# Moving small VectorE and GpSimd work between the eight steps of a round in a gated attention and expert kernel

## The chip, the cores and the metric

The kernel runs on one core of one Trainium2 chip. The metric is the device time of one launch in microseconds (us). The core has five engines that work from their own queues and wait for each other only at semaphores: TensorE (PE in the profile, with its weight loads shown as PEld), VectorE (DVE), ScalarE (ACT), GpSimd (POOL) and the sync engine (SP), which here only issues DMAs.

## What is computed

Each of 32 batches has 256 tokens of 128 features. Attention with a gated recurrent state comes first, then a feed-forward layer with one shared expert and eight routed ones, of which each token takes two. Both are modulated by a condition vector.

```python
h = layernorm(x) * (1 + ca) + sa
q, k, v = h @ W_q, h @ W_k, h @ W_v           # 16 heads of 64
a = sigmoid(h @ W_gate + b_gate)
# per head, token by token:
S = a_t[..., None] * S + k_t[..., None] * v_t[..., None, :]
o_t = einsum('bhk,bhkv->bhv', q_t, S)
x = x + ga * (o @ W_o)
h = layernorm(x) * (1 + cb) + sb
probs = sigmoid(h @ router_w.T + routing_bias)
scores, indices = top_k(probs, 2);  scores = scores / scores.sum()
x = x + gb * (shared_expert(h) + sum over the 2 chosen experts of score * expert(h))
```

## The kernel before

The program has two parts. The first, up to about 1000 us, does the attention of all batches and, behind it, the routing; the second multiplies the routed rows by the experts and adds everything up. The change touches the first part alone.

The first part is a loop over 16 rounds of two batches each. A round has eight **steps** (s = 0 to 7, `DUOS` = 4 to a batch); step number d = 8 i + s handles four heads of one batch. Rounds 0 to 2 and 15 are written out, and rounds 3 to 14 are one hardware loop. Each engine has its own function `round_of_steps`, and the order of its lines is the order in which that engine works: nothing reorders it. So a small operation that stands ahead of a large one delays it even where another engine waits for the large one.

What each engine does in a step s, in order:

- **PE**: `attend(d-1)` (the masked scores times the values, into `vo_bank`), `scores(d)` (into `score_banks`), the gate projection for step d+2 (`z_bank`), then in some steps a small product in `vo_bank` (the router in s = 0, transposes of the normalised input in s = 1 and 5, `ranks` in s = 4, transposes of the routed rows `new_rows` in s = 6 and 7), the query and key projections for step d+1 (`qk_banks`), `values` into `vo_bank`, and the output projection (`y_bank`).
- **DVE**: `first_head(d)` (two masked copies of scores into `A`, lines 1196 and 1198), `products(d+1)` (two multiplications of `qk_banks` by the scans, line 1188) and `scans(d+2)` (lines 1176 and 1181). Small work stands between them: `normalise`, `split_h` and `moments` for a coming batch, `moments2` and `normalise2` for the routed rows `new_rows`, and the routing of the two batches of the round before: `logits`, `choose`, `weigh`, `places`.
- **POOL**: `mask_second_head(d)` (the causal mask on the second head's half of `A`, line 510), `growth(d+1)` (line 600) and `gates(d+2)` (lines 593 and 595). Small work: `inverse_std`, `logits_exp`, `update_x`, `h_rows` (three operations on `new_rows` of one batch, from line 567) and `scatter_rows` (line 584: one indirect DMA for each of the eight parts of a round's routed rows).
- **ACT** copies PSUM results out, computes the gate's exponentials, and copies the second head's scores to `A`, behind which POOL masks them.

These waits of PE matter here. `attend(d-1)` waits until `first_head(d-1)` and `mask_second_head(d-1)` are done. `scores(d)` waits for `products(d)`. In s = 4 `values` overwrites `vo_bank`, in which the ranks lie, so it waits for `s_pos`, which DVE signals at line 1160, the second operation of `places`. In s = 6 and 7 the transposes wait for `h_rows`. On the other side `scatter_rows` waits for `s_dest`, the end of `places`, and `gates(d+2)` waits for `scans(d+1)`.

The lines of DVE that set the order in steps 3 to 5 are these (before):

```python
first_head(d)
if s == 3 and two:
    choose(i - 1)
if s == 5 and one:
    for u in range(2):
        normalise2((i - 1) * 2 + u, u, i)
if e == 0 and more:
    normalise(b * CHUNKS + CHUNKS, s_rs, b + 2, s_xn)
...
if s == 4 and two:
    places(i - 1)
if not (last and s == 2 * DUOS - 1):
    products(d + 1)
```

Of the kernel before, what the change touches and what calls it, by code (L numbers as in the profile page):

```python
# [20 lines left out]
ROUNDS = B // 2  # L21
# [21 lines left out]
def block_kernel(nc, x, W_q, W_k, W_v, W_gate, b_gate, W_o, shared_gate, shared_up, shared_down,  # L43
# [11 lines left out]
    with ctx:  # L55
# [442 lines left out]
        def _(pool):  # L498
# [120 lines left out]
            def round_of_steps(i, last):  # L619
                one = not (isinstance(i, int) and i < 1)  # L620
                two = not (isinstance(i, int) and i < 2)
                three = not (isinstance(i, int) and i < 3)
                for s in range(2 * DUOS):
                    half, e = s // DUOS, s % DUOS
                    b, d = i * 2 + half, i * 2 * DUOS + s
                    if e == 0 and not (last and half == 1):
                        inverse_std(b + 2)
                    if s == 0 and three:
                        scatter_rows(i - 2, s_fill, (i - 2) * 16, (6, 7))
                    if s in (1, 2) and two:  # L630
                        for n in range(2):
                            logits_exp(i - 1, (s - 1) * 2 + n)
                    if e == 3 and (half == 1 or one):
                        update_x(b - 1)
                    if s == 4 and one:
                        inverse_std2(i)
                    if s == 6 and one:
                        h_rows((i - 1) * 2 + 1, i - 1, 1, i)
                    if s >= 5 and two:
                        scatter_rows(i - 1, s_fill, (i - 1) * 16, ((0, 1), (2, 3), (4, 5))[s - 5])  # L640
                    mask_second_head(d)
                    if not (last and s == 2 * DUOS - 1):
                        growth(d + 1)
                    if not (last and s >= 2 * DUOS - 2):
                        gates(d + 2)
                    if s == 5 and one:
                        h_rows((i - 1) * 2, i - 1, 0, i)

            inverse_std(1)
            pool.wait_ge(s_wsplit, 4)  # L650
# [9 lines left out]
            with pool.Fori(3, ROUNDS - 1) as i:  # L660
                round_of_steps(i, False)
            round_of_steps(ROUNDS - 1, True)
            scatter_rows(ROUNDS - 2, s_fill, (ROUNDS - 2) * 16, (6, 7))
            update_x(B - 1)
            logits_exp(ROUNDS - 1, 0)
            inverse_std2(ROUNDS)
# [321 lines left out]
        def _(dve):  # L988
# [10 lines left out]
            def alone(semaphore, count):  # L999


                count = count if isinstance(count, int) else dve.to_reg(count)
                dve.wait_ge(s_ident, 1)
                dve.wait_ge(semaphore, count)  # L1004
# [142 lines left out]
                chosen(k, 6)  # L1147
                v.tensor_tensor(picked[:, :, :], pick[:, 0, :, :], pick[:, 1, :, :], ALU.add).then_inc(s_pick, 1)

            def places(k, where=dest):  # L1150

                def step(count):
                    alone(s_pl, (k - 1) * 3 + count)

                alone(s_rk, k)
                v.tensor_tensor(place_e[:, :, :], RANK[:, 0:PT * E].rearrange("p (n e) -> p n e", n=PT),
                                next_row[:, :].rearrange("p (a e) -> p a e", a=1).broadcast_to([P, PT, E]),
                                ALU.add).then_inc(s_pl, 1)
                step(1)
                v.tensor_tensor(next_row[:, :], next_row[:, :], RANK[:, PT * E:(PT + 1) * E], ALU.add).then_inc(s_pos, 1)  # L1160
                for t in range(TOP):
                    ins = v.tensor_tensor(place_k[:, t, :, :], pick[:, t, :, :], place_e[:, :, :], ALU.mult)
                ins.then_inc(s_pl, 1)
                step(2)
                v.tensor_reduce(place_f[:, :, :], place_k[:, :, :, :], AX.X, ALU.add).then_inc(s_pl, 1)
                step(3)
                alone(s_e0, k)
                v.tensor_copy(where[:, :], place_f[:, :, :].rearrange("p t n -> p (t n)")).then_inc(s_dest, 1)

            def scans(d):  # L1170

# [28 lines left out]
            def round_of_steps(i, last):  # L1200
                one = not (isinstance(i, int) and i < 1)
                two = not (isinstance(i, int) and i < 2)
                for s in range(2 * DUOS):
# [1 line left out]
                    b, d = i * 2 + half, i * 2 * DUOS + s  # L1205
                    more = not (last and half == 1)
                    first_head(d)
                    if s == 3 and two:
                        choose(i - 1)
                    if s == 5 and one:  # L1210
                        for u in range(2):
                            normalise2((i - 1) * 2 + u, u, i)
                    if e == 0 and more:
                        normalise(b * CHUNKS + CHUNKS, s_rs, b + 2, s_xn)
                    if s == 0 and two:
                        logits(i - 1)
                    if e == 1 and more:
                        split_h((1 - half) * T, b + 2)
                    if s == 4 and two:
                        places(i - 1)  # L1220
                    if not (last and s == 2 * DUOS - 1):
                        products(d + 1)
                    if s == 3 and two:
                        weigh(i - 2, i - 1)
                    if s == 3 and one:
                        moments2(b - 1, 1, i)
                    if s == 7:
                        moments2(b - 1, 0, i + 1)
                    if e == (3 if isinstance(b, int) and b == 0 else 2) and not last:
                        if isinstance(b, int) and b == 0:  # L1230
                            dve.wait_ge(s_x_rest, 16)
                        moments(b * CHUNKS + 2 * CHUNKS, b + 3)
# [703 lines left out]
```

## Time and profile before

| what | us |
|---|---|
| median of three timed runs (1334.47 to 1336.96) | 1336.66 |
| the profiled execution's own time | 1335.02 |
| its span, first to last instruction | 1332.9 |
| PE busy in the span | 1209.7 (91%) |
| DVE busy | 1039.1 (78%) |
| POOL busy | 946.5 (71%) |
| ACT busy | 717.1 (54%) |

Busy shares are means over both parts of the program. What a delay costs is seen only where an engine sits idle, in the round itself; the rows for that stand further down. A timeline row gives the start and the duration of one instruction, or of a few merged ones (x16), and in square brackets how long its engine had been idle before it and whose work ended the wait. Merged rows of pipelined instructions can overlap by a tenth of a microsecond.

### The profile page before, as it was taken

What the parts mean: (1) busy time and instruction counts of PE and PEld (TensorE: products, weight loads), DVE (VectorE), ACT (ScalarE), POOL (GpSimd) and SP (SyncE); (2) the same over time, 40 slices, a digit from 0 to 9 for tenths busy, and PEclk for the clock granted to TensorE, in tenths of its full rate; (3) what the DMA queues carried; (4) which work ended last, traced back from release to release, by engine and by line L of the source; (5) the groups of instructions that cost most, each with busy time, mean ns of one, the idle gap of its engine ahead of it and who ended that gap; (6) DMA issues with size and microseconds to landing.
All of it is one profiled execution on the core that took longest, in us unless ns stands there. A gap on an engine that the chain in (4) does not pass through costs nothing. (4 is left out here: it accounts for less than half of the span.)

```text
span 1332.9 us, 35442 instructions
## 1 busy us (share of the span) xinstructions
PE 1209.7 (91%) x10935; PEld 1063.2 (80%) x10935; DVE 1039.1 (78%) x2183; ACT 717.1 (54%) x1637; POOL 946.5 (71%) x1288
## 2 busy tenths in 40 slices
PE   5999999999999999998999999999989799999960
PEld 5888878888888878787888888887878688898850
DVE  7778788787878788888878787878766478887767
ACT  4666656556555556555555655655645345445420
POOL 4336687768696968778786969686876457777754
PEclk9999999999999999999999999999999999999995
DMA  8810202021120202020202112020202266666146
GB/s 247 240 69 2 90 22 87 25 85 58 47 98 7 101 8 97 10 95 20 85 24 85 63 42 101 4 101 8 99 26 92 70 189 193 191 178 182 61 155 224
DMA packets 88445, 119.30 MB, mean 90 GB/s; under 512 B 9652, under 2 KB 52327, under 8 KB 88384
## 3 DMA queue, kind: packets, MB, share of 16 engines
q1 hardware_dynamic: 79296, 101.47, 23.7%
q0 software_dynamic: 9088, 17.07, 3.7%
q8 instruction: 31, 0.51, 0.2%
q14 instruction: 30, 0.25, 0.1%
HBM read 50.29 MB, written 61.79 MB: 84 GB/s over the span
## 5 line engine op out<-in xcount | busy, mean ns | idle before, releaser
L1188 DVE TENSOR_TENSOR pairs<-qk_banks,pairs 128x512 f32<-128x512 f32 x256 | 164.5, 684 | 82.0 <-PE qk_banks L1537 81.5
L1638 PE MATMUL vo_bank<-A,shared 128*64 128x256 f32 (+1 forms) x2048 | 197.0, 335 | 27.5 <-POOL A L510 26.7
L710 POOL DMA_INDIRECT y_dram<-pairs,y_row x156 | 158.2, 1014 | 68.2 <-issue 43.9
L1176 DVE TENSOR_TENSOR_SCAN pairs<-pairs,shared 128x515 f32<-128x515 f32 x128 | 174.2, 1361 | 36.3 <-POOL pairs L593 30.1
L510 POOL TENSOR_SCALAR_AFFINE_SELECT A<-A 128x256 f32<-128x256 f32 x256 | 100.0, 416 | 136.3 <-ACT A L786 136.1
L1623 PE MATMUL score_banks<-pairs 64*128 64x128 f32 x2048 | 193.1, 286 | 3.2 <-ACT kx L779 3.2
L1638 PEld LDWEIGHTS vo_bank<-A,shared 128*64 128x64 f32 x2048 | 129.3, 138 | 81.7 <-issue 24.0
L1181 DVE TENSOR_TENSOR_SCAN pairs<-pairs,shared 128x515 f32<-128x515 f32 x128 | 167.8, 1311 | 0.0
L1623 PEld LDWEIGHTS score_banks<-pairs 64*128 64x128 f32 x2048 | 147.0, 189 | 25.7 <-issue 25.7
L584 POOL DMA_INDIRECT rows_dram<-token_rows,dest x120 | 124.9, 1041 | 58.3 <-issue 31.5
L767 ACT ACTIVATE shared<-vo_bank 128x512 f32<-128x512 f32 x128 | 76.5, 598 | 165.0 <-PE vo_bank L1638 165.0
L1535 PE MATMUL qk_banks<-h_hi,big 128*128 128x256 f32 x512 | 151.8, 297 | 0.0
L1537 PE MATMUL qk_banks<-h_hi,big 128*128 128x256 f32 x512 | 144.3, 282 | 0.0
L1649 PEld LDWEIGHTS y_bank<-wo,shared 128*128 128x128 f32 x1024 | 133.8, 191 | 13.1 <-ACT h_tile L792 1.1
L1536 PE MATMUL qk_banks<-h_lo,big 128*128 128x256 f32 x512 | 144.1, 281 | 0.0
L1649 PE MATMUL y_bank<-wo,shared 128*128 128x128 f32 x1024 | 135.1, 275 | 1.6 <-ACT h_tile L792 0.9
L758 ACT ACTIVATE shared<-vo_bank 128x512 f32<-128x512 f32 x128 | 76.5, 598 | 104.5 <-PE vo_bank L1580 104.5
L576 POOL TENSOR_TENSOR lg_e<-inv_e,lg 128x8 f32<-128x8 f32 x64 | 119.2, 1876 | 9.3 <-DVE lg L1115 9.3
L1196 DVE COPY_PREDICATED A<-causal,score_banks 128x512 f32<-128x512 int32 x128 | 93.7, 732 | 29.1 <-PE score_banks L1623 26.7
L746 ACT ACTIVATE pairs<-z_bank,neg_bg 128x256 f32<-128x256 f32 x256 | 107.6, 473 | 6.6 <-PE z_bank L1537 2.9
L785 ACT ACTIVATE A<-score_banks 128x256 f32<-128x256 f32 x128 | 49.2, 385 | 114.4 <-PE score_banks L1623 114.4
L752 ACT ACTIVATE pairs<-z_bank,half_bg 128x256 f32<-128x256 f32 x256 | 108.4, 486 | 0.0
(252 smaller groups left out, 3163.9 us busy)
## 6 DMA issues: line engine op xcount, KB each, us to landing
rows_dram<-pad_row SPq DMA_DIRECT2D x17, 2112.0 KB, 8.1
ga_all<-rows_dram SPq DMA_DIRECT2D x39, 264.0 KB
pairs<-y_dram SPq DMA_DIRECT2D x16, 512.0 KB
pairs<-in_L_ffn_gate_w_dram SPq DMA_DIRECT2D x39, 128.0 KB
pairs<-in_L_ffn_up_w_dram SPq DMA_DIRECT2D x39, 128.0 KB
ga_all<-in_L_ffn_down_w_dram SPq DMA_DIRECT2D x39, 128.0 KB, 2.2
mod_rows<-mod_rows_dram SPq DMA_DIRECT2D x32, 128.0 KB, 3.1
h_all<-h_tile SPq DMA_DIRECT2D x16, 256.0 KB, 2.3
```

The costliest lines, as they stand in the source:

```text
L576: g.tensor_tensor(lg_e[:, n, :], inv_e[:, n, :], lg[:, n, :], ALU.pow).then_inc(s_le, 1)
L584: g.indirect_dma_start(rows_dram, bass.IndirectOffsetOnAxis(ap=places[:, m:m + 1], axis=0), rows[:, m % PT, :], None, bounds_check=ROWS - ...
L710: g.indirect_dma_start(y_dram, bass.IndirectOffsetOnAxis(ap=y_row[:, u, n:n + 1], axis=0), y_out[:, u, n, :], None, bounds_check=TOKENS * ...
L1176: v.tensor_tensor_scan(G[:, 0:WIDE - 1], gi_t[:, 0:WIDE - 1], cap[:, 0:WIDE - 1], 1.0, ALU.mult, ALU.min)
L1181: v.tensor_tensor_scan(F[:, 0:WIDE - 1], ga_t[:, 0:WIDE - 1], restart[:, 0:WIDE - 1], 1.0, ALU.mult, ALU.add).then_inc(s_fg, 1)
L1188: v.tensor_tensor(out[:, :, :].rearrange("p u (c t) -> p u c t", c=CHUNKS), QKS[:, :, off:off + T].rearrange("p u (c t) -> p u c t", c=CHU ...
L1535: t.matmul(dst, hi, m_hi, start=True, stop=False)
L1536: t.matmul(dst, hi, m_lo, start=False, stop=False)
L1537: return t.matmul(dst, lo, m_hi, start=False, stop=True)
L1623: last = t.matmul(S[:, first:first + P], keys[rows, :], queries[rows, :], start=True, stop=True)
L1638: last = t.matmul(VO[h * DK:(h + 1) * DK, u * T + k * P:(u + 1) * T], v_sb[:, k, vcols], blocks.rearrange("p c t -> p (c t)"), start=(k == ...
L1649: last = t.matmul(Y[:, k * D:(k + 1) * D], oT[:, u * T + k * P:u * T + (k + 1) * P], wo[:, 2 * e + u, :], start=(e == 0 and u == 0 and k = ...
```

## The change

It moves work; no operation is added or left out, and a round still has eight scatters.

- On DVE, `places` is split into `rank_rows` (the two operations that read the ranks in PSUM and signal `s_pos`) and `destinations` (the rest). In s = 4 `rank_rows` stands right behind `first_head`, and `destinations` behind `products`. `normalise` and `split_h` go behind `products`, `logits` ahead of it. `choose` goes from s = 3, ahead of `products`, to s = 2, behind `products`. `normalise2` is split: one batch in s = 5 and the other in s = 6. `moments` for the first batch goes from s = 2 to s = 1.
- On POOL, the scatters, which stood two each in s = 5, 6, 7 and the next round's 0, are now three in s = 5, two in s = 6, none in s = 7, two in the next s = 0 and one in s = 1. `h_rows` of the second batch goes from the beginning of s = 6, ahead of the mask, to its end, behind the gates.
- Behind the last round three scatters are left in place of two.

The order of PE, ACT and SP is the same, instruction for instruction.

```diff
@@ -625,8 +625,8 @@
                     b, d = i * 2 + half, i * 2 * DUOS + s
                     if e == 0 and not (last and half == 1):
                         inverse_std(b + 2)
-                    if s == 0 and three:
-                        scatter_rows(i - 2, s_fill, (i - 2) * 16, (6, 7))
+                    if s < 2 and three:
+                        scatter_rows(i - 2, s_fill, (i - 2) * 16, ((5, 6), (7,))[s])
                     if s in (1, 2) and two:
                         for n in range(2):
                             logits_exp(i - 1, (s - 1) * 2 + n)
@@ -634,17 +634,15 @@
                         update_x(b - 1)
                     if s == 4 and one:
                         inverse_std2(i)
-                    if s == 6 and one:
-                        h_rows((i - 1) * 2 + 1, i - 1, 1, i)
-                    if s >= 5 and two:
-                        scatter_rows(i - 1, s_fill, (i - 1) * 16, ((0, 1), (2, 3), (4, 5))[s - 5])
+                    if s in (5, 6) and two:
+                        scatter_rows(i - 1, s_fill, (i - 1) * 16, ((0, 1, 2), (3, 4))[s - 5])
                     mask_second_head(d)
                     if not (last and s == 2 * DUOS - 1):
                         growth(d + 1)
                     if not (last and s >= 2 * DUOS - 2):
                         gates(d + 2)
-                    if s == 5 and one:
-                        h_rows((i - 1) * 2, i - 1, 0, i)
+                    if s in (5, 6) and one:
+                        h_rows((i - 1) * 2 + s - 5, i - 1, s - 5, i)
 
             inverse_std(1)
             pool.wait_ge(s_wsplit, 4)
@@ -660,7 +658,7 @@
             with pool.Fori(3, ROUNDS - 1) as i:
                 round_of_steps(i, False)
             round_of_steps(ROUNDS - 1, True)
-            scatter_rows(ROUNDS - 2, s_fill, (ROUNDS - 2) * 16, (6, 7))
+            scatter_rows(ROUNDS - 2, s_fill, (ROUNDS - 2) * 16, (5, 6, 7))
             update_x(B - 1)
             logits_exp(ROUNDS - 1, 0)
             inverse_std2(ROUNDS)
@@ -1147,17 +1145,20 @@
                 chosen(k, 6)
                 v.tensor_tensor(picked[:, :, :], pick[:, 0, :, :], pick[:, 1, :, :], ALU.add).then_inc(s_pick, 1)
 
-            def places(k, where=dest):
-
-                def step(count):
-                    alone(s_pl, (k - 1) * 3 + count)
+            def rank_rows(k):
 
                 alone(s_rk, k)
                 v.tensor_tensor(place_e[:, :, :], RANK[:, 0:PT * E].rearrange("p (n e) -> p n e", n=PT),
                                 next_row[:, :].rearrange("p (a e) -> p a e", a=1).broadcast_to([P, PT, E]),
                                 ALU.add).then_inc(s_pl, 1)
-                step(1)
+                alone(s_pl, (k - 1) * 3 + 1)
                 v.tensor_tensor(next_row[:, :], next_row[:, :], RANK[:, PT * E:(PT + 1) * E], ALU.add).then_inc(s_pos, 1)
+
+            def destinations(k, where=dest):
+
+                def step(count):
+                    alone(s_pl, (k - 1) * 3 + count)
+
                 for t in range(TOP):
                     ins = v.tensor_tensor(place_k[:, t, :, :], pick[:, t, :, :], place_e[:, :, :], ALU.mult)
                 ins.then_inc(s_pl, 1)
@@ -1166,6 +1167,10 @@
                 step(3)
                 alone(s_e0, k)
                 v.tensor_copy(where[:, :], place_f[:, :, :].rearrange("p t n -> p (t n)")).then_inc(s_dest, 1)
+
+            def places(k, where=dest):
+                rank_rows(k)
+                destinations(k, where)
 
             def scans(d):
 
@@ -1205,28 +1210,29 @@
                     b, d = i * 2 + half, i * 2 * DUOS + s
                     more = not (last and half == 1)
                     first_head(d)
-                    if s == 3 and two:
-                        choose(i - 1)
-                    if s == 5 and one:
-                        for u in range(2):
-                            normalise2((i - 1) * 2 + u, u, i)
+                    if s == 0 and two:
+                        logits(i - 1)
+                    if s == 4 and two:
+                        rank_rows(i - 1)
+                    if s in (5, 6) and one:
+                        normalise2((i - 1) * 2 + s - 5, s - 5, i)
+                    if not (last and s == 2 * DUOS - 1):
+                        products(d + 1)
+                    if s == 4 and two:
+                        destinations(i - 1)
                     if e == 0 and more:
                         normalise(b * CHUNKS + CHUNKS, s_rs, b + 2, s_xn)
-                    if s == 0 and two:
-                        logits(i - 1)
                     if e == 1 and more:
                         split_h((1 - half) * T, b + 2)
-                    if s == 4 and two:
-                        places(i - 1)
-                    if not (last and s == 2 * DUOS - 1):
-                        products(d + 1)
+                    if s == 2 and two:
+                        choose(i - 1)
                     if s == 3 and two:
                         weigh(i - 2, i - 1)
                     if s == 3 and one:
                         moments2(b - 1, 1, i)
                     if s == 7:
                         moments2(b - 1, 0, i + 1)
-                    if e == (3 if isinstance(b, int) and b == 0 else 2) and not last:
+                    if s == (6 if half else 3 if isinstance(b, int) and b == 0 else 1) and not last:
                         if isinstance(b, int) and b == 0:
                             dve.wait_ge(s_x_rest, 16)
                         moments(b * CHUNKS + 2 * CHUNKS, b + 3)
```

DVE, in rounds 3 to 14, from the `products` of step 2 to those of step 4, before (`lg_e` to `tsum` is `choose`, `place_e` and `next_row` are the ranks' reads, `dest` ends `places`, lines 1196 and 1198 are `first_head`):

```order
L1188 TENSOR_TENSOR pairs<-qk_banks,pairs 128x512 x2
...
L1124 TENSOR_SCALAR lg<-lg_e 128x32
...
L1134 TENSOR_TENSOR tsum<-top 128x4
L1188 TENSOR_TENSOR pairs<-qk_banks,pairs 128x512 x2
...
L1198 COPY_PREDICATED A<-causal,score_banks 128x256
L1020 TENSOR_SCALAR xn<-xs,mv,rstd 128x128 x2
L1156 TENSOR_TENSOR place_e<-vo_bank,next_row 128x32
L1160 TENSOR_TENSOR next_row<-next_row,vo_bank 128x8
...
L1168 CAST dest<-place_f 128x8
L1188 TENSOR_TENSOR pairs<-qk_banks,pairs 128x512 x2
```

and now:

```order
L1193 TENSOR_TENSOR pairs<-qk_banks,pairs 128x512 x2
L1122 TENSOR_SCALAR lg<-lg_e 128x32
...
L1132 TENSOR_TENSOR tsum<-top 128x4
...
L1193 TENSOR_TENSOR pairs<-qk_banks,pairs 128x512 x2
...
L1203 COPY_PREDICATED A<-causal,score_banks 128x256
L1151 TENSOR_TENSOR place_e<-vo_bank,next_row 128x32
L1155 TENSOR_TENSOR next_row<-next_row,vo_bank 128x8
L1193 TENSOR_TENSOR pairs<-qk_banks,pairs 128x512 x2
...
L1169 CAST dest<-place_f 128x8
```

`choose` has moved behind the `products` of step 2, the reads of the ranks stand directly behind `first_head`, and `normalise` has left the place between them.

POOL, in the same rounds, from the scatters of step 5 to the mask of step 7, before (`new_rows<-token_ids` begins an `h_rows`, `y_sb` and `xs` are `update_x`, `AFFINE_SELECT` is the mask):

```order
L584 DMA rows_dram<-token_rows,dest 73216x132 x2
...
L510 AFFINE_SELECT A<-A 128x2x128 x2
...
L567 COPY new_rows<-token_ids 128x2
...
L584 DMA rows_dram<-token_rows,dest 73216x132 x2
...
L510 AFFINE_SELECT A<-A 128x2x128 x2
...
L617 TENSOR_TENSOR xs<-xs,y_sb 128x256
L584 DMA rows_dram<-token_rows,dest 73216x132 x2
...
L510 AFFINE_SELECT A<-A 128x2x128 x2
```

and now:

```order
L584 DMA rows_dram<-token_rows,dest 73216x132 x3
...
L510 AFFINE_SELECT A<-A 128x2x128 x2
...
L567 COPY new_rows<-token_ids 128x2
...
L584 DMA rows_dram<-token_rows,dest 73216x132 x2
...
L510 AFFINE_SELECT A<-A 128x2x128 x2
...
L567 COPY new_rows<-token_ids 128x2
...
L617 TENSOR_TENSOR xs<-xs,y_sb 128x256
...
L510 AFFINE_SELECT A<-A 128x2x128 x2
```

Ahead of the mask of step 5 there is one scatter more; the second `h_rows` (in the first list it stands right behind the one shown, among the rows left out) has crossed the mask of step 6; and ahead of the mask of step 7 there is `update_x` alone.

## Rows read from the trace of the kernel before

**Rows 1.** Waits, all of PE: line, waited for, us, times, longest us.

```profile
PE vo_bank L1638 <- POOL A L510: 26.7, 27, 2.4
PE vo_bank L1578 <- DVE next_row L1160: 25.0, 14, 2.2
```

**Rows 2.** Windows, one round: length, busy us of each engine, clock, DMA.

```profile
497.10:558.70 61.60, 57.78 (x579) 50.77 (x577) 50.20 (x105) 36.20 (x89) 47.80 (x69) 1.00 0.16 57
```

**Rows 3.** Timeline of PE, `attend` at the steps' starts: start, duration, [idle].

```profile
528.28 1.52 PE L1638 MATMUL vo_bank<-A,shared 128*64 128x256 f32 x16
535.19 1.52 PE L1638 MATMUL vo_bank<-A,shared 128*64 128x256 f32 x16
...
542.81 0.50 PE L1578 MATMUL vo_bank<-big,h_hi 128*128 128x512 f32 x1 [1.94 <-DVE next_row L1160]
544.59 1.52 PE L1638 MATMUL vo_bank<-A,shared 128*64 128x256 f32 x16
...
551.73 1.52 PE L1638 MATMUL vo_bank<-A,shared 128*64 128x256 f32 x16
...
560.17 1.52 PE L1638 MATMUL vo_bank<-A,shared 128*64 128x256 f32 x16 [1.25 <-POOL A L510]
...
568.01 1.52 PE L1638 MATMUL vo_bank<-A,shared 128*64 128x256 f32 x16 [0.64 <-POOL A L510]
575.81 1.52 PE L1638 MATMUL vo_bank<-A,shared 128*64 128x256 f32 x16
...
582.95 1.30 PE L1638 MATMUL vo_bank<-A,shared 128*64 128x256 f32 x12
```

**Rows 4.** Timeline of DVE, steps 2 to 4 of the same round.

```profile
526.90 1.29 DVE L1188 TENSOR_TENSOR pairs<-qk_banks,pairs 128x512 f32<-128x512 f32 x2 [1.28 <-PE qk_banks L1537]
...
529.08 1.34 DVE L1176 TENSOR_TENSOR_SCAN pairs<-pairs,shared 128x515 f32<-128x515 f32 x1
...
532.42 0.41 DVE L1124 TENSOR_SCALAR lg<-lg_e 128x32 f32<-128x32 f32 x1
...
534.56 1.28 DVE L1188 TENSOR_TENSOR pairs<-qk_banks,pairs 128x512 f32<-128x512 f32 x2
...
540.21 0.72 DVE L1196 COPY_PREDICATED A<-causal,score_banks 128x512 f32<-128x512 int32 x1
...
541.14 1.25 DVE L1020 TENSOR_SCALAR xn<-xs,mv,rstd 128x128 f32 x2
...
542.59 0.16 DVE L1160 TENSOR_TENSOR next_row<-next_row,vo_bank 128x8 f32<-128x8 f32 x1
```

**Rows 5.** Timeline of POOL, from step 5 to the next round's step 1.

```profile
544.46 1.09 POOL L584 DMA_INDIRECT rows_dram<-token_rows,dest  x1 [2.14 <-DVE dest L1168]
...
548.71 0.77 POOL L510 TENSOR_SCALAR_AFFINE_SELECT A<-A 128x256 f32<-128x256 f32 x2 [1.88 <-ACT A L786]
...
551.45 0.18 POOL L567 COPY new_rows<-token_ids 128x2 f32 x1
...
556.85 1.04 POOL L584 DMA_INDIRECT rows_dram<-token_rows,dest  x1 [0.25 <-issue]
...
559.16 0.77 POOL L510 TENSOR_SCALAR_AFFINE_SELECT A<-A 128x256 f32<-128x256 f32 x2
...
561.23 1.69 POOL L614 TENSOR_TENSOR y_sb<-y_sb,ga_all 128x256 f32<-128x256 f32 x1
...
566.99 0.79 POOL L510 TENSOR_SCALAR_AFFINE_SELECT A<-A 128x256 f32<-128x256 f32 x2
...
569.17 1.03 POOL L549 TENSOR_SCALAR veps<-mv 128x2 f32<-128x2 f32 x1
...
576.61 4.20 POOL L576 TENSOR_TENSOR lg_e<-inv_e,lg 128x8 f32<-128x8 f32 x2
...
583.05 3.33 POOL L576 TENSOR_TENSOR lg_e<-inv_e,lg 128x8 f32<-128x8 f32 x2
```

**Rows 6.** Tile `dest`, all scatters from it: duration ns min/median/max.

```profile
L584 POOL DMA_INDIRECT rows_dram<-token_rows,dest x120: 966/1010/1952, 173.7 to 1043.6; - x120
```

## Prediction

> **What bounds the kernel now.** I read the waits of PE first, since PE is the busiest engine. Two waits stand out: the causal mask of the second head, from POOL, holds `attend` up for 26.7 us in 27 places, and the ranks' read, from DVE, holds `values` up for 25.0 us in 14 places [rows 1]. Together they are 51.7 us. Then I read one round in windows: it lasts 61.6 us, of which PE works 57.8, DVE 50.2 and POOL 47.8 [rows 2]. So PE bounds the round, with holes, and a hole that is closed shortens the round as long as DVE and POOL keep up. The timeline of PE shows where the holes are: 1.94 us in step 4, 1.25 at the beginning of step 7 (the mask of step 6 is late) and 0.64 at the beginning of the next step 0 (the mask of step 7) [rows 3]. That is 3.83 us a round. A reader should see in the same rows how long a step takes without its hole: 6.91 us for step 3, 9.40 - 1.94 = 7.46 for step 4, 7.14 for step 5, 8.44 - 1.25 = 7.19 for step 6, 7.84 - 0.64 = 7.20 for step 7, 7.80 for step 0 and 7.14 for step 1. These are the deadlines against which the moved work is set.
>
> **The ranks' read on DVE.** PE wants to go on at 542.81 - 1.94 = 540.87, which is 5.68 us into step 4; the read ends at 542.59 + 0.16 = 542.75 [rows 3, 4]. `first_head` ends where `normalise` begins, at 541.14. `normalise` then takes 1.25 us, with the two reads behind it [rows 4]. Taking it away alone gives an end near 541.14 + 0.44 = 541.58, so 0.7 us of the wait would stay. The rest has to come from `choose`. It takes 534.56 - 532.42 = 2.14 us ahead of the `products` of step 3 [rows 4]. In step 2 it now stands behind `products`, which end at 526.90 + 1.29 = 528.19. There it replaces `moments`, which took until 529.08, so the scans begin at 530.33, or 1.25 us later, and `first_head` of step 3 ends at 532.42 + 1.25 = 533.67. PE has the next projection ready one step after 526.90, at 533.81. So `products` of step 3 start at 533.81 in place of 534.56, and all behind them comes 0.75 us earlier. `first_head` of step 4 ends at 540.39, the reads at 540.83, and PE wants them at 540.87. This closes the wait with nothing to spare; if `choose` takes longer there, as it may beside other POOL work, the excess over 533.81 - 533.67 = 0.14 comes back in every round.
>
> **The masks on POOL.** Ahead of the mask of step 6 POOL now does two scatters and no `h_rows`, ahead of that of step 7 `update_x` without scatters, but the mask of step 5 gets three scatters, and step 1 one. POOL has little rest here, so I add up the whole row of work in the new order, with durations from its timeline [rows 5]: a scatter is half of 559.16 - (556.85 - 0.25) = 2.56, so 1.28; a mask 0.77, and mask, growth and gates together 561.23 - 559.16 = 2.07, or 569.17 - 566.99 = 2.18 in step 7 and after; an `h_rows` half of 556.60 - 551.45 = 5.15, so 2.58; `update_x` 566.99 - 561.23 - 2.56 = 3.20; the work from `inverse_std` to the mask of step 0, 576.61 - 569.17 - 2.18 = 5.26, which includes two scatters; a first pair of `logits_exp` 583.05 - 576.61 - 2.18 = 4.26. PE starts `attend` 560.17 - (559.16 + 0.77) = 0.24 after the mask [rows 3, 5], so a mask must end 0.24 before its step does.
>
> The row begins when the places are known. `products` of step 4 run from 5.70 to 6.95, and from the end of the ranks' read to the first scatter it takes 544.46 - 542.75 = 1.71 [rows 4, 5], which now is counted from the end of `products`: 8.66 us into step 4, or 1.20 into step 5. Then, each time in us from the beginning of the step named:
> - Step 5: scatters to 5.04, mask to 5.81; it is wanted at 6.90. Gates to 7.11, `h_rows` to 9.69.
> - Step 6: that is 2.55. Two scatters to 5.11, mask to 5.88 (wanted 6.95), gates to 7.18, second `h_rows` to 9.76.
> - Step 7: 2.57. `update_x` to 5.77, mask to 6.54 (wanted 6.96), gates to 7.95.
> - Step 0: 0.75. `inverse_std` and two scatters to 6.01, mask to 6.78 (wanted 7.56), gates to 8.19.
> - Step 1: 0.39. Scatter to 1.67, `logits_exp` to 5.93, mask to 6.70 (wanted 6.90).
>
> So no mask comes late, with 0.20 us to spare at the worst. The 1.88 us that POOL idled ahead of the mask of step 5 [rows 5] is what pays for it: the third scatter goes in there. The `h_rows` of each batch end about 2.6 us into the step in which PE transposes them, behind `attend` and the scores; before, the first batch was ready 551.45 + 2.58 - 551.73 = 2.30 us into step 6, and PE shows no wait for it among its two, so I count that as free with its cover of scores and gate projection. If it slips by more than a microsecond, PE waits there.
>
> **The rest.** `normalise`, `split_h` and the second `normalise2` move behind work that PE or POOL wants sooner; PE uses their results in the next step at the earliest, so I count them at nothing, and DVE at 50.2 of 57.8 us still has room. The later scatters delay the copy into `token_rows` on SP and the loads and padding queued behind it by about one step; the copy is wanted by ACT in step 4, some three steps later. The third scatter behind the last round costs 1.28 us on POOL, which I take as hidden, since the shared expert's products come first on PE.
>
> **A rule on the shared port.** The scatters take 1.01 us at the median and once 1.95 [rows 6], and `update_x` shows 1.69 us for one operation [rows 5]. [...]
>
> **The sum.** All of the two waits: 51.7 us. Left over per round: at least 0 by the margins above, at most about 0.5 for either side together if something is slowed as far as the next rows show; I take 0.2, nearer to the margins, over the 13 rounds (2 to 14) that show both masks: 2.6. In the last round the steps are shorter and the mask waits up to 2.4 us [rows 1]; an estimate of 1.0 stays. The profiled execution took 1335.02: 1335.02 - 51.7 + 2.6 + 1.0 = 1286.9. The median of the runs is 1.64 above that execution, so the forecast is 1288.5, and its own range 1283 to 1294.
>
> **The rivals.**
> - A, POOL becomes the bound. For it: five scatters lie ahead of the mask of step 7 and three stand beside scans, with only 0.42 and 0.20 us to spare. If two of them take 1.95 [rows 6], 2 x 0.94 - 0.42 = 1.5 us a round come back; if one does, 0.5. With 1.0 on average: 1336.66 - 51.7 + 13 + 1 = 1299, at most 1305.5. Against it: the median.
> - B, the ranks stay late because `choose` stretches beside POOL's gates and `update_x`. With 0.5 us more a round: 1288.5 + 6.5 = 1295.
> - C, slower: three scatters ahead of the mask of step 5 hold `attend` up. The mask would have to end 1.1 + 3.8 = 4.9 us later than I have it for the gain to be gone, so the scatters would have to take 2.9 us each, against 1.95 at the longest [rows 6]. With 3.5 each: 13 x (6.7 - 4.9) = 23 us slower, 1360.
> - D, nothing happens: DVE proves the bound, its 50.2 us stretched by waits to about 61 a round; then 1336.
>
> **How the numbers follow.** My forecast gets 0.65, A 0.20, B 0.08, C 0.03, D 0.04. The first three are all faster: 0.93. About 0.2% is what can be told from no change, some 2.7 us: same 0.04, slower 0.03. The range goes from 1282 (everything closed, and the first matmul after a wait, 0.50 us [rows 3], a little shorter) to 1301, which takes in B and more than half of A.
>
> **What would show it.** In the profile after, the wait of `values` for the ranks should be near zero; if 0.3 us or more stands there in each round, the step on `choose` was wrong. The waits of `attend` for the mask should be gone at the beginning of steps 7 and 0; if they reappear at step 2 or 0, the row of POOL's work was too short. POOL should begin the mask of step 5 without idling. A round should last 57.8 to 58.3 us. A new wait of PE for `h_rows` or for `products` would make the prediction wrong in a place that I counted at nothing.

## The result and the profile after

The changed kernel takes 1298.33 us (median of 4 runs, 1295.9 to 1302.46), the kernel before 1336.81 beside it: a ratio of 0.9715, 95% interval 0.9689 to 0.9741. The forecast was 1288.5, so the gain is 38 us where 48 was expected. The time lies inside the stated range, but 4 us above the forecast's own part of it (1283 to 1294): it is covered only because the range was widened for rivals A and B. The profiled execution of after took 1295.9 with a span of 1294.1, against 1332.9 for the span before.

The waits of PE in after that answer to [rows 1] (line, waited for, us in total, times, longest us):

```profile
PE vo_bank L1538 <- issue: 9.2, 14, 1.2
...
PE vo_bank L1644 <- POOL A L510: 4.8, 14, 0.7
...
PE vo_bank L1584 <- DVE next_row L1155: 0.3, 1, 0.3
```

The mask's wait has fallen from 26.7 us to 4.8, the ranks' from 25.0 us to one case of 0.3. In their place there is a new one: 9.2 us at the transposes of `new_rows` (line 1538). So 14.3 of 51.7 us are left.

One round of after, from `attend` at the start of one step 7 to the next, against the 61.6 us of [rows 2] (columns: length, busy us of PE, PEld, DVE, ACT, POOL, granted clock, DMA share, GB/s; the window has 60 us):

```profile
540.00:600.00 60.00, 59.04 (x594) 51.51 (x590) 49.45 (x104) 35.95 (x88) 47.62 (x72) 1.00 0.17 58
```

The holes are in the timeline of PE: the starts of steps 4, 5, 6 and 7, the transposes in step 7, and the start of the next step 7 (start, duration, [idle before it]):

```profile
517.49 1.52 PE L1644 MATMUL vo_bank<-A,shared 128*64 128x256 f32 x16
...
525.01 1.52 PE L1644 MATMUL vo_bank<-A,shared 128*64 128x256 f32 x16
...
532.15 1.52 PE L1644 MATMUL vo_bank<-A,shared 128*64 128x256 f32 x16
...
539.67 1.52 PE L1644 MATMUL vo_bank<-A,shared 128*64 128x256 f32 x16 [0.32 <-POOL A L510]
...
544.25 0.41 PE L1538 MATMUL vo_bank<-ident,new_rows 128*128 128x128 f32 x2 [0.62 <-issue]
...
598.52 1.52 PE L1644 MATMUL vo_bank<-A,shared 128*64 128x256 f32 x16 [0.31 <-POOL A L510]
```

A round lasts 598.52 - 539.67 = 58.85 us. What is left in it is 0.31 for the mask of step 6 and 0.62 at the transposes, 0.93 together where 3.83 stood. Both come from POOL, whose timeline over the same stretch reads:

```profile
526.31 1.75 POOL L584 DMA_INDIRECT rows_dram<-token_rows,dest  x1 [2.41 <-DVE dest L1169]
528.37 0.98 POOL L584 DMA_INDIRECT rows_dram<-token_rows,dest  x1 [0.30 <-issue]
529.65 0.97 POOL L584 DMA_INDIRECT rows_dram<-token_rows,dest  x1 [0.30 <-issue]
530.62 0.79 POOL L510 TENSOR_SCALAR_AFFINE_SELECT A<-A 128x256 f32<-128x256 f32 x2
...
533.98 1.47 POOL L571 TENSOR_TENSOR new_rows<-new_rows,mod_rows 128x256 f32<-128x256 f32 x1
535.60 1.79 POOL L584 DMA_INDIRECT rows_dram<-token_rows,dest  x1 [0.15 <-issue]
...
538.66 0.77 POOL L510 TENSOR_SCALAR_AFFINE_SELECT A<-A 128x256 f32<-128x256 f32 x2
...
540.70 0.18 POOL L567 COPY new_rows<-token_ids 128x2 f32 x1
540.85 1.69 POOL L569 TENSOR_TENSOR new_rows<-new_rows,mod_rows 128x256 f32<-128x256 f32 x1
542.68 1.47 POOL L571 TENSOR_TENSOR new_rows<-new_rows,mod_rows 128x256 f32<-128x256 f32 x1
544.11 0.73 POOL L614 TENSOR_TENSOR y_sb<-y_sb,ga_all 128x256 f32<-128x256 f32 x1
...
545.73 0.77 POOL L510 TENSOR_SCALAR_AFFINE_SELECT A<-A 128x256 f32<-128x256 f32 x2
...
549.38 1.17 POOL L584 DMA_INDIRECT rows_dram<-token_rows,dest  x1 [0.36 <-issue]
```

Beside the 2.41 us for which POOL stands before the first scatter, it hardly rests. The mask of step 6 is done at 538.66 + 0.77 = 539.43, 7.28 us into a step that begins at 532.15. The second `h_rows` is done at 544.15, and PE begins its transposes 0.1 us later. The profile names no releaser for that wait (`issue`); that it is `h_rows` is borne out by e4 below, where `h_rows` ends earlier and the wait is gone. The same stretch of DVE shows what runs beside the long instructions:

```profile
523.00 0.16 DVE L1155 TENSOR_TENSOR next_row<-next_row,vo_bank 128x8 f32<-128x8 f32 x1
...
525.23 0.17 DVE L1169 CAST dest<-place_f 128x8 int32<-128x8 f32 x1
...
525.93 1.23 DVE L1181 TENSOR_TENSOR_SCAN pairs<-pairs,shared 128x515 f32<-128x515 f32 x1
527.07 1.20 DVE L1186 TENSOR_TENSOR_SCAN pairs<-pairs,shared 128x515 f32<-128x515 f32 x1
...
534.84 1.69 DVE L1186 TENSOR_TENSOR_SCAN pairs<-pairs,shared 128x515 f32<-128x515 f32 x1
...
540.27 1.75 DVE L1181 TENSOR_TENSOR_SCAN pairs<-pairs,shared 128x515 f32<-128x515 f32 x1 [0.34 <-POOL pairs L593]
541.94 1.69 DVE L1186 TENSOR_TENSOR_SCAN pairs<-pairs,shared 128x515 f32<-128x515 f32 x1
...
548.41 1.23 DVE L1181 TENSOR_TENSOR_SCAN pairs<-pairs,shared 128x515 f32<-128x515 f32 x1
```

A scatter that starts while a scan is under way ends some 0.9 us after that scan: the first at 528.06, 0.90 after its scan (527.16), the fourth at 537.39, 0.86 after its scan (536.53), the one of step 0 at 550.55, 0.91 after its scan (549.64). So its length depends on how much of the scan is left when it starts: the first and the fourth take 1.75 and 1.79 us, the one of step 0 only 1.17. The scatters of these rows with no scan under way at their start take 0.97 or 0.98. The scans beside scatters are not slowed: 1.23 and 1.20 us in step 5. The two operations of `h_rows` beside the scans of step 7 take 1.69 and 1.47 us; 0.73 is what `update_x`, an operation of the same form, takes right behind them, with no scan beside it. These scans suffer too: 1.75 and 1.69 us instead of 1.23 and 1.20. In before the first scatter of a round starts a little ahead of the scan, at 544.46 in [rows 5], and takes 1.09 us:

```profile
544.78 1.22 DVE L1176 TENSOR_TENSOR_SCAN pairs<-pairs,shared 128x515 f32<-128x515 f32 x1
```

In after the places are ready only behind `products`, and the first scatter starts 0.38 us behind the start of the scan: this moves it from the short kind to the long one.

### The profile page after: what moved, and what is told of

The parts are those of the page before. It is cut to its first block and busy times, and to the rows that moved or that the text cites. A ratio compares the mean times of both kernels' runs of the same rounds, so it can differ in the third digit from the quotient of the medians.

```text
span 1294.1 us, 35439 instructions
## 1 busy us (share of the span) xinstructions
PE 1209.5 (93%) x10935; PEld 1062.2 (82%) x10935; DVE 1017.3 (79%) x2183; ACT 713.5 (55%) x1637; POOL 925.3 (72%) x1288
## 5 line engine op out<-in xcount | busy, mean ns | idle before, releaser
L584 POOL DMA_INDIRECT rows_dram<-token_rows,dest x120 | 142.1, 1184 | 66.9 <-issue 36.1
L576 POOL TENSOR_TENSOR lg_e<-inv_e,lg 128x8 f32<-128x8 f32 x64 | 115.3, 1819 | 10.8 <-DVE lg L1113 10.4
```

The lines of the kernel that those rows point to most:

```text
L576: g.tensor_tensor(lg_e[:, n, :], inv_e[:, n, :], lg[:, n, :], ALU.pow).then_inc(s_le, 1)
L584: g.indirect_dma_start(rows_dram, bass.IndirectOffsetOnAxis(ap=places[:, m:m + 1], axis=0), rows[:, m % PT, :], None, bounds_check=ROWS - ...
```

## The experiments

All are edits of after unless something else is said. Ratios are against the kernel before in the same job; after itself, run again beside e5 to e7, gave 1299.96 us, 0.9711 (0.9693 to 0.9728), with the same two waits (9.0 and 5.1 us).

> The changed kernel once more, beside the others on one chip: 1296 to 1302, with 0.3 us a round for the mask of step 6 and 0.6 for the transposes of step 7.

**e4: destinations first.** DVE works out the destinations ahead of `products` of step 4, so that the scatters can start earlier; nothing of POOL is changed.

```diff
-                    if not (last and s == 2 * DUOS - 1):
-                        products(d + 1)
                     if s == 4 and two:
                         destinations(i - 1)
+                    if not (last and s == 2 * DUOS - 1):
+                        products(d + 1)
```

> The changed kernel with destinations ahead of products in step 4 (behind the reads of the ranks), so that the scatters' rows are known 1.2 us earlier. Theory (the chain on POOL is late because it begins late): the first scatter starts at about step 5's start and out of the scans' way, both waits close, products of step 4 start 0.9 us later at no cost to PE: 1298.3 - 12 = 1285 to 1289. Rival (POOL's begin does not matter, h_rows waits for the scans of its own step): the 0.62 us for the transposes stay, 1293 to 1298. If products become late for scores instead, a new wait of PE at its scores or for kx shows.

Measured: 1281.86 us, 0.9585 (0.9564 to 0.9606). In the loop PE shows no wait for the mask or the transposes, and one of 0.2 us for the ranks in its first round; the last round, behind the loop, keeps one wait for the mask:

```profile
PE vo_bank L1644 <- POOL A L510: 0.9, 1, 0.9
```

The starts of steps 5, 6 and 7 on PE in this kernel:

```profile
518.80 1.52 PE L1644 MATMUL vo_bank<-A,shared 128*64 128x256 f32 x16
...
525.94 1.52 PE L1644 MATMUL vo_bank<-A,shared 128*64 128x256 f32 x16
...
533.07 1.52 PE L1644 MATMUL vo_bank<-A,shared 128*64 128x256 f32 x16
```

and its POOL in the same stretch:

```profile
518.71 1.09 POOL L584 DMA_INDIRECT rows_dram<-token_rows,dest  x1 [1.01 <-DVE dest L1169]
...
526.57 0.72 POOL L571 TENSOR_TENSOR new_rows<-new_rows,mod_rows 128x256 f32<-128x256 f32 x1
527.56 2.01 POOL L584 DMA_INDIRECT rows_dram<-token_rows,dest  x1 [0.26 <-issue]
...
530.84 0.83 POOL L510 TENSOR_SCALAR_AFFINE_SELECT A<-A 128x256 f32<-128x256 f32 x2
```

with DVE's first scan of step 5:

```profile
519.55 1.23 DVE L1181 TENSOR_TENSOR_SCAN pairs<-pairs,shared 128x515 f32<-128x515 f32 x1
```

The first scatter starts 0.09 us before step 5 does, 1.39 earlier in the step than in after. `h_rows` of the first batch now runs ahead of the scans: its last operation takes 0.72 us in place of 1.47. A scatter begun beside a scan still takes 2.01, but the first one now starts ahead of the scans and takes 1.09. The mask of step 6 is done 531.67 - 525.94 = 5.73 us into the step, against 7.28, and the prediction's 5.88. So the row of POOL's work is what was left in after, and its start decides. Run again beside e8 and e9 it gave 1282.17, 0.96 (0.9584 to 0.9617): some 15 to 17 us less than after, and the fastest kernel here.

> The changed kernel with destinations ahead of products once more, on another chip: 1280 to 1286 and no wait of PE within the loop.

**e3: one scatter less ahead of the mask of step 5.** The scatters of steps 5 to 7 go two, two, one.

```diff
-                    if s in (5, 6) and two:
-                        scatter_rows(i - 1, s_fill, (i - 1) * 16, ((0, 1, 2), (3, 4))[s - 5])
+                    if s >= 5 and two:
+                        scatter_rows(i - 1, s_fill, (i - 1) * 16, ((0, 1), (2, 3), (4,))[s - 5])
```

> The changed kernel with its scatters two, two and one in steps 5, 6 and 7 (three, two, none before), and two and one in the next steps 0 and 1 as in the changed kernel. Theory (a chain on POOL that begins with three scatters and runs without rest to the second h_rows makes PE wait 0.31 us for the mask of step 6 and 0.62 us for the transposes of step 7): one scatter of 1.27 us less ahead of both closes both waits, and the mask of step 7, which now has 0.87 us to spare, is 0.1 to 0.4 us late: 1298.3 - 13 x (0.92 - 0.25) = 1288 to 1292. Rival (what makes the chain long is the scans beside h_rows, not the third scatter): within 3 us of the changed kernel, 1295 to 1301.

Measured: 1289.65 us, 0.9632 (0.9612 to 0.9652). Both waits of after are gone; `attend` waits a little for the mask of step 7, ahead of which the fifth scatter now stands. PE's timeline at the start of a step 0:

```profile
542.56 1.52 PE L1644 MATMUL vo_bank<-A,shared 128*64 128x256 f32 x16 [0.22 <-POOL A L510]
```

**e6: e3 and e4 together.**

> The changed kernel with both mends: destinations ahead of products in step 4, and scatters two, two and one in steps 5, 6 and 7. Theory (with the places known early PE has no wait left in the loop, so more room on POOL is worth nothing): the same as with the places alone, 1280 to 1284. Rival (POOL still takes time from DVE or PE): 1276 to 1280; if the scatter in step 7 makes its mask late, 1284 to 1288.

Measured: 1288.52 us, 0.9629 (0.9615 to 0.9642). PE's waits in this kernel:

```profile
PE vo_bank L1644 <- POOL A L510: 3.1, 13, 0.4
```

The gains don't add up: e6 is no faster than e3, and slower than e4 alone; a round of the loop lasts 58.0 us in e6 and e3, 57.7 in e4. With the earlier start the third scatter has room in step 5, and a scatter in step 7 only makes the mask of step 7 late. The three, two, none of the change is the better spread once the destinations come earlier. In the traces the first part of the program is 4 us longer in e6 than in e4; what else their medians differ by, some 2 us, is not explained.

**e9: the scatters of before**, two each in steps 5, 6, 7 and 0, with everything else of after.

```diff
-                    if s < 2 and three:
-                        scatter_rows(i - 2, s_fill, (i - 2) * 16, ((5, 6), (7,))[s])
+                    if s == 0 and three:
+                        scatter_rows(i - 2, s_fill, (i - 2) * 16, (6, 7))
...
-                    if s in (5, 6) and two:
-                        scatter_rows(i - 1, s_fill, (i - 1) * 16, ((0, 1, 2), (3, 4))[s - 5])
+                    if s >= 5 and two:
+                        scatter_rows(i - 1, s_fill, (i - 1) * 16, ((0, 1), (2, 3), (4, 5))[s - 5])
...
-            scatter_rows(ROUNDS - 2, s_fill, (ROUNDS - 2) * 16, (5, 6, 7))
+            scatter_rows(ROUNDS - 2, s_fill, (ROUNDS - 2) * 16, (6, 7))
```

> The changed kernel with the scatters spread as before (two each in steps 5, 6, 7 and the next 0). Theory: the two waits of 0.92 us a round go with the third scatter of step 5, as with two, two and one, and the mask of step 7, now behind two scatters, is 1.0 to 1.6 us late: 1299 to 1307. Rival (the spread of the scatters is what freed the masks): 1310 or more.

Measured: 1302.72 us, 0.9753 (0.9738 to 0.9768). The start of a step 0 on PE:

```profile
551.54 1.52 PE L1644 MATMUL vo_bank<-A,shared 128*64 128x256 f32 x16 [1.49 <-POOL A L510]
```

The two waits of after are gone, and the mask of step 7 is late by 1.49 us, 21.3 us in 15 times, against after's 14.3. So the new spread in after takes off a third of these 21.3 us (7) and moves the rest to other places.

**e5: `choose` back in step 3**, ahead of `products`.

```diff
+                    if s == 3 and two:
+                        choose(i - 1)
...
-                    if s == 2 and two:
-                        choose(i - 1)
```

> The changed kernel with choose back in step 3 ahead of products. Theory on the ranks (choose is worth 0.75 us of the 1.93, normalise the rest): a wait of 0.7 us a round of values for the ranks comes back, 9 us in all, while POOL's waits of 0.92 us a round stay as they are or shrink by what the later step 5 gives them: 1298 + 5 to 10 = 1303 to 1308, if the granted TensorE clock stays at its full level in the loop. Rival (a wait is charged twice, because the clock falls to its half level behind it in every round, as in the run with POOL's changes alone): 1320 or more. Rival (normalise alone was the cause): no wait for the ranks, 1296 to 1300.

Measured: 1307.54 us, 0.9785 (0.9763 to 0.9807), 7.6 above after in the same job. PE's timeline in step 4:

```profile
529.65 0.50 PE L1584 MATMUL vo_bank<-big,h_hi 128*128 128x512 f32 x1 [0.77 <-DVE next_row L1155]
```

The ranks' wait is back at 0.77 us, 10.3 in 14 times. The prediction had 0.75 for `choose` and the rest of the 1.94 for `normalise`. That rest, 1.17 us, comes from the difference alone: no run moves only `normalise`.

**e1 and e7: DVE's part alone.** e1 has DVE of after and POOL of before. e7 differs in one thing: both batches' `normalise2` stay in step 5, as before.

```diff
-                    if s in (5, 6) and one:
-                        normalise2((i - 1) * 2 + s - 5, s - 5, i)
+                    if s == 5 and one:
+                        for u in range(2):
+                            normalise2((i - 1) * 2 + u, u, i)
```

> Only the changes on DVE are made; POOL's order is that of before. Theory (the two waits are separate, and POOL's row of work is what is left in the changed kernel): the ranks' wait of 1.93 us a round goes, the mask waits at steps 7 and 0 stay or grow a little, since the scatters begin some 1.4 us later in step 5: 1336.8 - 25 + 0 to 8 = 1312 to 1320, with 25 to 35 us of mask waits in the trace. Rival (POOL's row sets the period of the round, so time won on DVE comes back as mask waits): 1330 to 1337, with 45 us or more of mask waits.

> The changes on DVE without the split of normalise2 (both batches in step 5, as before), with POOL's order of before. Theory (the 3.75 us for the mask of step 6 in the run with all of DVE's changes alone came from POOL standing at the second h_rows for a normalise2 that DVE now does a step later): POOL no longer idles 4.25 us there, the wait for the ranks is gone, and the masks of steps 6 and 7 are late by 1.5 to 2.5 us a round in all: 1312 to 1322. Rival (any DVE change alone is slower, since the later places push POOL's row): mask waits of 3 us and more, 1330 to 1365.

Measured: e1 1364.59 us, 1.0192 (1.0169 to 1.0215), slower than before by 25 us, outside both expectations; e7 1303.09 us, 0.974 (0.9723 to 0.9756), better than expected. What happens in e1 stands in the timelines of POOL and PE around the mask of step 6:

```profile
567.51 0.19 POOL L567 COPY new_rows<-token_ids 128x2 f32 x1 [4.25 <-DVE new_rows L1109]
...
571.83 0.78 POOL L510 TENSOR_SCALAR_AFFINE_SELECT A<-A 128x256 f32<-128x256 f32 x2
...
572.85 2.83 PE L1646 MATMUL vo_bank<-A,shared 128*64 128x256 f32 x16 [3.75 <-POOL A L510]
```

and in the window behind it (granted clock third from the end):

```profile
572.80:576.00 3.20, 3.15 (x20) 2.08 (x22) 2.55 (x2) 0.28 (x1) 3.00 (x4) 0.50 0.00 0
```

In before's order the second `h_rows` stands ahead of the scatters and the mask of step 6. With `normalise2` of the second batch moved to step 6 on DVE, POOL stands still for 4.25 us there, and the two scatters and the mask wait behind it; `attend` comes 3.75 us late (54.2 us in 15 times), and then runs at the lower clock level, 1.2 GHz: 2.83 us for what takes 1.52. PE's two waits together are only 2.7 us more than the 51.7 of before (54.2, and 0.2 for the ranks); the rest of the 25 us fits this lower clock, which the trace shows behind the wait in every round of the loop. In e7 the ranks' wait is gone and the mask's wait is 17.7 us in 20 times, less than the 26.7 of before though POOL's order is the same: step 6 lasts 8.4 to 8.6 us, as before, in five of the loop's twelve rounds, and 7.3 to 7.7 in the others. Why the rounds differ stays open. So nearly all of the gain, 0.974 of 0.9711, is had with DVE's moves alone, as long as `normalise2` isn't split.

**e8: the opposite cut.** After, with the second `h_rows` back ahead of the mask of step 6 and both `normalise2` in step 5.

```diff
+                    if s == 6 and one:
+                        h_rows((i - 1) * 2 + 1, i - 1, 1, i)
...
-                    if s in (5, 6) and one:
-                        h_rows((i - 1) * 2 + s - 5, i - 1, s - 5, i)
+                    if s == 5 and one:
+                        h_rows((i - 1) * 2, i - 1, 0, i)
...
```

The edit of `normalise2`, left out here, is the one shown for e7.

> The changed kernel with the second h_rows back ahead of the mask of step 6 and both normalise2 back in step 5. Theory (the masks are late by what stands ahead of them on POOL): the 0.6 us for the transposes of step 7 go, and the mask of step 6 is 2.2 to 2.9 us late in place of 0.31: 1298 + 13 x 1.6 = 1316 to 1325 at full TensorE clock, up to 1345 if the clock falls behind such a wait in every round. Rival (the ranks' wait was all that counted): 1298 to 1304.

Measured: 1333.85 us, 0.9982 (0.9968 to 0.9997): nearly the whole gain is gone. A start of step 7 on PE:

```profile
556.71 1.89 PE L1647 MATMUL vo_bank<-A,shared 128*64 128x256 f32 x16 [2.31 <-POOL A L510]
```

The mask's waits come to 32.7 us in 14 times, 18.4 more than what is left in after; `attend` behind them takes 1.89 us in place of 1.52, and that lower clock fits the rest of the loss. So three scatters in step 5 and an `h_rows` ahead of the mask of step 6 don't fit together. The split of `normalise2` and the move of `h_rows` are one move with two halves: with the first half alone the kernel is slower than before by 25 us (e1). What leaving out both halves costs depends on the scatters: with three, two, none the gain is gone (e8, 0.9982), with the scatters of before nearly all of it stays (e7, 0.974). The new scatters without the pair lose what DVE's moves win; the pair without the new scatters (e9, 0.9753) is no faster than neither (e7); both together add 0.3% to e7 (0.9711).

**e2: POOL's part alone**, with DVE of before.

> Only the changes on POOL are made; DVE's order is that of before. Theory: the ranks' wait of 1.93 us a round stays, the mask waits go, since the scatters begin at step 5's start as before and POOL has 1.9 us more a round; no wait of more than 0.3 us a round for the second h_rows: 1336.8 - 26.7 = 1310 to 1314. Rival (h_rows of the second batch, moved behind the gates and beside the scans, is late by itself): 0.6 us a round or more of waits at the transposes of step 7, 1318 or more.

Measured: 1325.74 us, 0.9901 (0.988 to 0.9922). The masks' waits, 26.7 us before, are gone but for one of 1.1, and `h_rows` finds its input in time; the ranks' wait is 25.0 us in 14 times as before. But only 13 us come out. PE's timeline behind that wait:

```profile
540.97 0.55 PE L1576 MATMUL vo_bank<-big,h_hi 128*128 128x512 f32 x1 [1.94 <-DVE next_row L1158]
...
544.01 1.84 PE L1636 MATMUL vo_bank<-A,shared 128*64 128x256 f32 x16
```

and the windows over it:

```profile
541.00:543.00 2.00, 2.00 (x7) 1.75 (x8) 1.78 (x7) 0.59 (x2) 0.39 (x1) 0.57 0.00 0
543.00:545.00 2.00, 2.00 (x14) 1.50 (x14) 2.00 (x3) 0.58 (x3) 1.67 (x2) 0.57 0.10 34
```

For 4 us the granted clock is 0.57, PE busy all the time. At full speed that work would have taken 0.57 x 4 = 2.28 us, so up to 1.7 us are lost. The trace has such a stretch in ten of the loop's twelve rounds: enough for the 13 us that are missing.

## Why the prediction was right, and where it was not

- **The bound and the two holes.** Right. PE bounds the round, and the time that went is the time of the two waits: 37.4 of the 39.1 us between the two profiled executions. The other 1.7 fit a stretch of lower clock that before has once in the loop (355 to 365 us) and after does not.
- **The ranks' read.** Right to 0.1 us. The read was put 5.64 us into step 4 and ends 523.16 - 517.49 = 5.67 into it. The price of `choose`, 0.75, is 0.77 in e5. The rival of a stretched `choose` did not come.
- **The start of POOL's row.** Right: the first scatter was put 1.20 us into step 5 and starts 526.31 - 525.01 = 1.30 into it.
- **The masks, step by step.** Here it failed. The row of durations was carried from the places of before to those of after, as if each operation had a length of its own. Mask of step 6: predicted done 5.88 us into its step and wanted at 6.95, measured 7.28. Second `h_rows`: predicted done 2.57 us into step 7, measured 544.15 - 539.67 = 4.48. From first scatter to mask of step 5 it takes 4.31 us in place of 3.84, from the end of the first `h_rows` to the mask of step 6 538.66 - 535.45 = 3.21 in place of 2.56, and the second `h_rows` 3.45 in place of 2.58. These first two are 1.12 of the 1.40 us by which the mask of step 6 is later than forecast. The change put the second `h_rows` where `update_x` had stood, right behind the gates that release DVE's scans, and let scatters start inside scans; there they are stretched. So `update_x`, priced at 3.20, takes 1.67 in after (544.11 to 545.78), and the mask of step 7, which the prediction thought the tightest but one, has 0.9 us to spare.
- **"If it slips by more than a microsecond, PE waits there."** That cover was named, counted at nothing, and it gave way: `h_rows` slipped by 1.9 us, and PE waits 0.62 at the transposes, 9.2 us in all. The prediction's own signs of being wrong there came: a new wait of PE for `h_rows`, and a round of 58.85 us where 57.8 to 58.3 was forecast. The cover should have been carried into the sum with the scatters' rival, since one shift moves both.
- **The sum.** The left-over was put at 0.2 us a round, 2.6 + 1.0 = 3.6 in all; it is 0.93 a round and 14.3 in all. That is 10.7 too little, against 1.7 from the clock, and the medians add 0.8: 9.8 us, the whole miss.
- **The rivals.** POOL as the bound was the right mechanism, and its price of 1.0 us a round and 1299 us the right size (0.93 and 1298.3); its place was not. It was put at the mask of step 7 and came at the mask of step 6 and the transposes. It should have had the larger chance: the 1.69 us of `update_x` beside scans stood in [rows 5].
- **The shared port.** The median of all scatters, 1.01 us in [rows 6], was the argument for short ones, and it failed: in before, of 78 scatters between 300 and 900 us, only 9 start inside a scan, with 0.15 us of it left at most, while in after, of the 82 that start between 300 and 900 us, 31 start inside a scan, take 1.13 to 1.79 us and end 0.85 to 0.92 us after that scan. The Trainium skill, "SBUF — State Buffer", section "SBUF: two separate sides", says that a DVE operation with two SBUF inputs and a GpSimd operation that reads SBUF exclude each other, and that the one that starts first has the port for its whole instruction. The trace agrees in part: the two scans and the two operations of `h_rows` in step 7 take 3.88 us together (540.27 to 544.15), and alone one behind the other they would take 1.23 + 1.20 + 2 x 0.73 = 3.89; but the first scan is lengthened although it starts first. That GpSimd cannot write the descriptors of its DMAs the same section says of DVE operations in a 2-port mode; whether that is what holds the scatters here, no run shows. That it is the port at all, and not another thing that scans bring, is argued and not shown.

What is shown is the role of POOL's row: one scatter less ahead (e3) and an earlier start (e4) each close both waits, though e3 opens a smaller one for the mask of step 7.

## What to carry to other kernels

The length of a small operation belongs to its place, not to the operation: when two pieces of work change places, price each with the rows of the place it moves to, and above all what will stand beside the other engine's long two-input operations. A move on one engine can need its other half on another engine: look for the instruction on the second engine that waits for the moved result, and for what is queued behind it. When an engine that feeds the bound one has no rest left in a stretch, look for what starts that stretch: starting it 1.4 us earlier was worth more than any spreading of its parts that was tried (e3, e6, e9).

## What the runs showed of the hardware

- **The clock behind a wait is not the same from kernel to kernel.** The wait of 1.94 us of PE for the ranks is followed by the lower level nearly every round in e2, but in before, with the same wait in each round, only once in the loop: its window 500 to 600, with one such wait and three for the masks, has a granted clock of 1.00, and 355 to 360 has 0.80. Behind 0.77 us (e5) and 1.49 us (e9) the clock stays at 1.00 in the loop. Which difference in the work ahead of the wait decides was not found; it stays open.

The windows of before:

```profile
355.00:360.00 5.00, 3.53 (x21) 2.79 (x23) 4.67 (x12) 1.18 (x3) 2.56 (x4) 0.80 0.04 14
...
500.00:600.00 100.00, 95.55 (x961) 84.15 (x960) 81.09 (x171) 59.24 (x143) 78.18 (x111) 1.00 0.18 67
```

- **A scan and an elementwise POOL operation slow each other.** In step 7 of after both scans are at 1.75 and 1.69 us instead of 1.23 and 1.20, and the two POOL operations beside them at 1.69 and 1.47 instead of 0.73.
- **A scatter begun inside a scan waits for the end of that scan, not for the next scan.** It ends 0.85 to 0.92 us after the first (the 31 such scatters of after), while the second scan, which starts meanwhile, is not slowed (527.07, 1.20 us in after). One begun 0.32 us ahead of a scan takes 1.09 (544.46 in before).
- **From the end of `dest` on DVE to the first scatter on POOL 0.9 us pass** (525.40 to 526.31 in after), though POOL stands waiting and the trace shows nothing else that it waits for.
